# Normalisation of four batches and the turning of two gated weights, moved into the last steps of the head loop

## What is computed

```python
x = x + _L0_attn_ref(_layernorm(x, axis=-1), L0_attn_w_qkv, L0_attn_w_o)      # 16 heads of 128, softmax
x = x + _L0_xattn_ref(_layernorm(x, axis=-1), ctx_2048, ctx_2048, ...)        # linear attention over a context
x = x + _L0_ffn_ref(_layernorm(x, axis=-1), weight1, weight2, weight3)        # gated, NF4 weights
x = x + _L1_attn_ref(_layernorm(x, axis=-1))                                  # over the features
x = x + _L1_xattn_ref(_layernorm(x, axis=-1), ctx_2048, mask_BxS2_bk0, ...)   # masked, gated
x = x + _L1_ffn_ref(_layernorm(x, axis=-1), L1_ffn_c_fc, L1_ffn_c_proj)       # ternary weights
```

```python
q_prime = jax.nn.relu(jnp.einsum('bhnd,fd->bhnf', q, Wqf))
out = jnp.einsum('bhmf,bhfe->bhme', q_prime, kv) / (jnp.einsum('bhmf,bhf->bhm', q_prime, k_sum)[..., None] + 1e-08)
return out.transpose(0, 2, 1, 3).reshape(B, Sq, H) @ Wo.T + bo
```

## Time and profile before

| | |
|---|---|
| median of 3 runs | 932.9 us (932.67 to 932.92) |
| the profiled execution | 934.24 us, its span 932.4 us |
| PE busy | 858.7 us (92% of the span), 6868 matmuls |
| DVE busy | 729.2 us (78%) |
| ACT busy | 520.5 us (56%) |
| POOL busy | 369.0 us (40%) |
| mean granted clock of PE | 0.98 of 2.4 GHz |
| the two parts | DVE's last update of X ends at 564.65 us, ACT's last copy at 567.31 us; the second part's first instruction is at 568.66 us |

### The profile page before, as it was taken

The page is one execution under the profiler, slowest core; times in us unless marked ns, Lnnn a source line. Parts: engine busy times, 40 slices in busy tenths (PEclk is TensorE's granted clock), DMA queues, the critical chain, the costliest instruction groups (busy, mean ns, idle before and its releaser), DMA issues. The chain is left out here.

```text
span 932.4 us, 18697 instructions
## 1 busy us (share of the span) xinstructions
PE 858.7 (92%) x6868; PEld 637.5 (68%) x6868; DVE 729.2 (78%) x1777; ACT 520.5 (56%) x1245; POOL 369.0 (40%) x356
## 2 busy tenths in 40 slices
PE   4798998999999999999999986999988889999786
PEld 3455766777777777777777765787856568777554
DVE  5738867878888788887887745898798879887895
ACT  1435576656665566656665643554364863535556
POOL 3104455545555555545554553044133031522410
PEclk9889999999999999999999997999999999999999
DMA  9022331011101111011100000000000010000001
GB/s 285 32 65 68 55 93 35 2 35 34 34 7 27 34 34 34 0 34 34 34 5 6 1 1 1 1 2 1 1 2 1 1 46 2 1 1 1 1 1 46
DMA packets 34722, 25.56 MB, mean 27 GB/s; under 512 B 9492, under 2 KB 31596, under 8 KB 34668
## 3 DMA queue, kind: packets, MB, share of 16 engines
q1 hardware_dynamic: 34380, 24.56, 10.1%
q10 hardware_dynamic: 288, 0.26, 0.1%
HBM read 22.65 MB, written 2.17 MB: 27 GB/s over the span
## 5 line engine op out<-in xcount | busy, mean ns | idle before, releaser
L476 POOL CAST exp_hi<-exp_scores 128x1024 f16<-128x1024 f32 x64 | 67.0, 1047 | 217.9 <-ACT exp_scores L580 217.9
L74 PE MATMUL banks<-value_out_hi,xn_t_hi 128*128 128x256 f16 x512 | 140.8, 275 | 2.3 <-DVE X L874 2.3
L478 POOL TENSOR_TENSOR exp_lo<-exp_scores,exp_hi 128x1024 f16<-128x1024 f32 x64 | 140.7, 2198 | 5.1
L580 ACT ACTIVATE exp_scores<-banks,exp_bias,unscale 128x256 f32<-128x256 f32 x256 | 141.0, 560 | 2.1
L75 PE MATMUL banks<-value_out_lo,xn_t_hi 128*128 128x256 f16 x512 | 140.6, 275 | 0.0
L76 PE MATMUL banks<-value_out_hi,xn_t_lo 128*128 128x256 f16 x512 | 140.6, 275 | 0.0
L1064 PE MATMUL banks<-qk 128*128 128x256 f32 x512 | 122.7, 383 | 9.9 <-ACT exp_scores L580 9.9
L1064 PEld LDWEIGHTS banks<-qk 128*128 128x128 f32 x512 | 97.2, 191 | 31.4 <-issue 10.5
L874 DVE SCALAR_TENSOR_TENSOR X<-banks,colsum,X 128x256 f32<-128x256 f32 x256 | 106.2, 477 | 11.0 <-DVE colsum L865 9.6
L562 ACT ACTIVATE qk<-banks 128x512 f32<-128x512 f32 x128 | 75.8, 601 | 59.1 <-PE banks L76 59.1
L853 DVE TENSOR_REDUCE neg_rowmax<-banks 128x4 f32<-128x1024 f32 x64 | 78.1, 1221 | 31.4 <-PE banks L1064 31.4
(11 more groups left out here) (238 smaller groups left out, 1965.9 us busy)
## 6 DMA issues: line engine op xcount, KB each, us to landing
head_weights<-in_wqkv_d SPq DMA_DIRECT2D x32, 128.0 KB, 3.7
weight_absmax_rows<-across_partitions SPq DMA_DIRECT2D x15, 256.0 KB, 4.1
X<-in_x_d SPq DMA_DIRECT2D x4, 512.0 KB, 7.5
head_weights<-in_wqkvt_d SPq DMA_DIRECT2D x16, 128.0 KB, 3.4
head_weights<-in_w_o_d SPq DMA_DIRECT2D x16, 128.0 KB, 3.5
out<-X SPq DMA_DIRECT2D x8, 256.0 KB, 2.1
res_then_ternary_then_kv<-in_c_fc_d SPq DMA_DIRECT2D x1, 1024.0 KB, 6.5
res_then_ternary_then_kv<-in_c_proj_d SPq DMA_DIRECT2D x1, 1024.0 KB, 8.2
```

The lines of the kernel that those rows point to most:

```text
L74: nc.tensor.matmul(out, lhs[0], rhs[0], start=first, stop=False)
L476: nc.gpsimd.tensor_copy(probh[:, s1_.par], prob[:, s1_.par]).then_inc(exph_ready, 1)
L478: nc.gpsimd.tensor_tensor(probl[:, s1_.par], prob[:, s1_.par], probh[:, s1_.par], ALU.subtract).then_inc(expl_ready, 1)
L580: last = nc.scalar.activation(prob[:, s1_.par, t, :], sc_ps[t // ST][:, t % ST, :], ACT.Exp, bias=nbias[:, t:t + 1], scale=unscale[:, s1_. ...
```

## The change

Two pieces of work go into the last iterations of the head loop.

1. **Normalisation of batches 0 to 3 for the linear attention.** Pair 0 is final after iteration 62, pair 1 after iteration 63. DVE: statistics of pair 0 in iteration 63 between the reciprocals and the row maxima, its four normalised tiles behind the row maxima; statistics of pair 1 in iteration 64 behind the row maxima, its tiles in iteration 65 between the reciprocals and the column sums. POOL: the powers, on 128x4, at the end of its iterations 62 and 63. The normalised tiles go into `ctxt` and `k0t`, which are free by then. PE turns pair 0 at the end of iteration 64 and pair 1 in iteration 65 between value pass and column sums, eight turns each, into banks 6 and 2. ACT copies each pair with two copies into `g.first_xt`, new room behind kv0's halves. The second part starts with lin_q for streams 0 to 3; the lists of turns leave out their seven stages (`EARLY`), and the waits count from the fifth batch. POOL's addition of bo needs no wait for these four.
2. **The gated weights.** PE turns pieces 0 and 1 in iteration 64 ahead of the scores and pieces 2 and 3 behind the column sums, ahead of the turns of pair 0. ACT copies 0 and 1 ahead of the bias and the exps of that iteration, 2 and 3 behind the copies of pair 0. (The title's "two weights" are w1 and w2.) w3 stays behind the loop, in banks 0 and 1 instead of 2 and 3.

```diff
+EARLY = [f"lin_{part}" for part in ("stats", "aggr", "eps", "pow", "xn", "turn", "xt")]
...
+    first_xn = [t[:, :, :].rearrange("p k n -> p (k n)").rearrange("p (t d) -> p t d", d=D) for t in (ctxt, k0t)]
+    LAST = STEPS - 1
+    FIRST_A, FIRST_B = 6, 2
...
+            for p in range(STREAMS // 2):
+                if known(i) and i == LAST - 1 + p:
+                    pool.wait_ge(early_eps, p + 1)
+                    rows = slice(TP * p, TP * (p + 1))
+                    nc.gpsimd.tensor_tensor(rstd[:, rows], rstd[:, rows], g.neg_half[:, rows], ALU.pow).then_inc(
+                        early_rstd, 1)
...
+            if known(i) and i == LAST + 1:
+                gated_weights(0)
+                gated_weights(1)
             if runs(i, 1):
                 s1_ = Step(i, c - 1)
                 act.wait_ge(nmax_ready, i)
...
+            if known(i) and i == LAST + 1:
+                first_rows(0)
+                gated_weights(2)
+                gated_weights(3)
...
+        def first_rows(p):
+            act.wait_ge(early_full, p + 1)
+            for a in range(2):
+                last = nc.scalar.activation(g.first_xt[2 * p + a],
+                                            bank[(FIRST_A, FIRST_B)[a]].rearrange("p (k n) -> p k n", k=KT), ACT.Copy)
+            last.then_inc(early_xt, 1)
...
+        run(act, step)
+        first_rows(1)
...
+        def first_statistics(p):
+
+            tiles = range(TP * p, TP * (p + 1))
+            dve.wait_ge(x_added, STEPS - NP + p + 1)
+            for t in tiles:
+                nc.vector.bn_stats(stats[:, t, :], g.X[:, t, :]).then_inc(early_stats, 1)
+            dve.wait_ge(early_stats, TP * (p + 1))
+            for t in tiles:
+                nc.vector.bn_aggr(mv[:, t, :], stats[:, t, :]).then_inc(early_aggr, 1)
+            dve.wait_ge(early_aggr, TP * (p + 1))
+            nc.vector.tensor_scalar(rstd[:, TP * p:TP * (p + 1)], mv[:, TP * p:TP * (p + 1), 1], LN_EPS, None,
+                                    ALU.add).then_inc(early_eps, 1)
+
+        def first_rows(p):
+
+            dve.wait_ge(early_rstd, p + 1)
+            for t in range(TP * p, TP * (p + 1)):
+                last = nc.vector.tensor_scalar(first_xn[p][:, t - TP * p, :], g.X[:, t, :], mv[:, t, 0:1],
+                                               rstd[:, t:t + 1], ALU.subtract, ALU.mult)
+            last.then_inc(early_xn, 1)
...
+        def first_rows(p):
+
+            pe.wait_ge(early_xn, p + 1)
+            if p:
+                pe.wait_ge(early_xt, p)
+            else:
+                pe.wait_ge(exp_ready, STEPS)
+            for a in range(2):
+                for t in range(ST):
+                    for k in range(KT):
+                        last = nc.tensor.transpose(bank[(FIRST_A, FIRST_B)[a]][:, k * S + t * P:k * S + (t + 1) * P],
+                                                   first_xn[p][:, a * ST + t, k * P:(k + 1) * P], g.ident[:, :])
+            last.then_inc(early_full, 1)
...
-        pe.wait_ge(lv, ROUNDS * 8 * STEP_OPS)
...
         for q in range(2):
+            pe.wait_ge(wt_ready, 3 + q)
...
-                    last = nc.tensor.transpose(bank[2 + q].bitcast(BF16)[0:rows, at:at + P], src, g.identb[:, :])
+                    last = nc.tensor.transpose(bank[q].bitcast(BF16)[0:rows, at:at + P], src, g.identb[:, :])
...
+    lin_xt = [g.first_xt[b] if b < STREAMS else xt[b] for b in R]
...
+    nl = [b + 1 - STREAMS for b in R]
+    nth_norm = lambda layer, b: nl[b] if layer == "lin" else n[b]
...
-                pe.wait_ge(lin["xt_ready"], n[s])
-                features_first(PB[s], g.wq0, xt[s]).then_inc(lin_q_full, 1)
+                if s >= STREAMS:
+                    pe.wait_ge(lin["xt_ready"], nl[s])
+                features_first(PB[s], g.wq0, lin_xt[s]).then_inc(lin_q_full, 1)
...
+    early = [i for i in range(len(work)) if names[i] in EARLY]
+    done = {(b, i): 0.0 for b in range(STREAMS) for i in early}
+    nth = {(b, e): sum(engine[i] == e for i in early) if b < STREAMS else 0 for b in range(B) for e in ENGINES}
```

More of the change, by code:

```diff
@@ L270, in attention_part @@
     tround, tclamp, tdone = sem("ternary_rounded"), sem("ternary_clamped"), sem("ternary_done")
+    early_stats, early_aggr, early_eps = sem("first_rows_stats"), sem("first_rows_mean"), sem("first_rows_eps")
+    early_rstd, early_xn = sem("first_rows_rstd"), sem("first_rows_xn")
+    early_full, early_xt = sem("first_rows_turned"), sem("first_rows_xt")
+    first_xn = [t[:, :, :].rearrange("p k n -> p (k n)").rearrange("p (t d) -> p t d", d=D) for t in (ctxt, k0t)]
+    LAST = STEPS - 1
+    FIRST_A, FIRST_B = 6, 2
     NF_REP = 12
@@ L595, in step, with gated_weights @@
                                          bias=-ROUND).then_inc(tdone, 1)
-        run(act, step)
-        for w in range(4):
+        def first_rows(p):
[4 more added lines that the diff above has]
+            last.then_inc(early_xt, 1)
+        def gated_weights(w):
             act.wait_ge(wt_full, w + 1)
@@ L607, in _ @@
                 last = nc.scalar.activation(g.w3t[0:rows, k, :],
-                                            bank[2 + q].bitcast(BF16)[0:rows, k % 3 * D:(k % 3 + 1) * D], ACT.Copy)
+                                            bank[q].bitcast(BF16)[0:rows, k % 3 * D:(k % 3 + 1) * D], ACT.Copy)
             last.then_inc(wt_ready, 1)
@@ L842, in step @@
                     nc.vector.reciprocal(rhl[:, s2.par, :, 0], rowsum[:, s2.par, :]).then_inc(rrh_ready, 1)
+            if known(i) and i == LAST:
+                first_statistics(0)
+            if known(i) and i == LAST + 2:
+                first_rows(1)
             if preps(i, c, 2):
@@ L853, in step @@
                 nc.vector.tensor_reduce(nmax[:, :], sc_both, AX.X, ALU.max, negate=True).then_inc(nmax_ready, 1)
+            if known(i) and i == LAST:
+                first_rows(0)
+            if known(i) and i == LAST + 1:
+                first_statistics(1)
             if known(i) and i == 0:
@@ L1432, in norm_stage @@
             elif part == "xn":
[L1433 removed]
+                dve.wait_ge(ln["rstd"], nth_norm(layer, s))
                 for t in range(ST):
@@ L1787, in turns_by_engine @@
     free = {e: 0.0 for e in ENGINES}
-    nth = {(b, e): 0 for b in range(B) for e in ENGINES}
-    done = {}
+    early = [i for i in range(len(work)) if names[i] in EARLY]
+    done = {(b, i): 0.0 for b in range(STREAMS) for i in early}
+    nth = {(b, e): sum(engine[i] == e for i in early) if b < STREAMS else 0 for b in range(B) for e in ENGINES}
     turns = {e: [] for e in ENGINES}
-    for _ in range(B * len(work)):
+    for _ in range(B * len(work) - STREAMS * len(early)):
         best = None
@@ L1851, in decoder @@
     g.kv0 = sb("kv0", [P, B, XH // 2, 34])
-    g.shared = sb("features_then_ternary_then_kv0", [P, 2, F2 * KT])
-    flat = g.shared[:, :, :].rearrange("p a n -> p (a n)").bitcast(F16)
+    halves = B * XH * 17
+    g.many = sb("features_then_ternary_then_kv0_and_rows", [P, halves + STREAMS * KT * S])
+    g.shared = g.many[:, 0:2 * F2 * KT].rearrange("p (a n) -> p a n", a=2)
+    flat = g.many[:, 0:halves].bitcast(F16)
+    g.first_xt = [g.many[:, halves + b * KT * S:halves + (b + 1) * KT * S].rearrange("p (k n) -> p k n", k=KT)
+                  for b in range(STREAMS)]
     g.kvh, g.kvl = (flat[:, n * B * XH * 17:(n + 1) * B * XH * 17].rearrange("p (b j c) -> p b j c", j=XH // 2, c=34)
```

39 lines of the change are left out of this document (20 added, 19 removed).

## The result

The changed kernel takes **921.72 us** (median of 5 runs, 921.54 to 923.28) against 932.9 us before (932.67 to 933.83). The ratio is 0.989, with a 95% interval of 0.9875 to 0.9905: faster by 11.2 us, where 8.7 were forecast. The profiled execution took 921.72 us, its span is 919.9 us.

A forecast was written before the change was run, and what follows sets the result against it. ACT's late w3 copies, then PE up to lin_f1, bound the seam; first part 1.65 us earlier, lin_f1 ending at 579.4 against 588.16, 8.75 us gained: median 924.2 us from 932.9, range 922.4 to 926.8.

The forecast's parts named there:

- What bounds the seam: ACT's w3 copies end the first part last; then PE idles 6.98 us behind DVE's statistics and bounds until lin_f1.
- Iteration 63, +0.3: DVE's pair 0 statistics, 2.2 us in 1.96 us of waiting, move row maxima through ACT's exps by +0.3 us.
- Iteration 64, +0.8: Second statistics, 2.25 us behind the row maxima, make DVE's column sums and PE's last value pass 0.8 us late.
- The value pass, -1.7: PE's last value pass runs at 2.4 GHz because turns fill the gap before it: 1.7 us gained.
- Rival B: Clock lost in the loop's tail too, or low longer behind the barrier: 6.7 us gained, 926.2 us; chance 0.17.
- Iteration 65: DVE's first tensor_scalar waits for POOL's exp_lo; ACT's copies end at 565.65, the first part 1.65 us earlier.
- The barrier, 1.35: Between the parts, from ACT's last copy to DVE's first instruction, the barrier costs 1.35 us.
- The second part: First lin_q matmul at 567.2, 12.2 us of PE to the end of lin_f1 at 579.4: 8.75 us earlier.
- the loss of 1.7: Behind the barrier PE runs 3.4 us at half clock, losing 1.7 us, +0.3 against before.
- The sum: Whole kernel: handover 8.75 us earlier, span 923.7, median 924.2 us.
- from there the same distance to the end (343.6 us): From the handover to DVE to the end of the kernel nothing changes: 343.6 us as before.
- Rival C: Clock does not fall across the barrier: 1.7 us more, 10.4 gained, 922.5 us; chance 0.12.

The follow-up runs named there:

- experiment 4: Changed kernel with pair 0's four bn_stats done twice in iteration 63, first into a spare tile; 924.18 us.
- experiment 5: Changed kernel with pair 1's four tiles normalised on ACT instead of by DVE's four tensor_scalar; 922.53 us.
- experiment 1: The kernel before, unedited, run and traced a second time; 931.26 us.
- experiments 5 and 6: For experiment 5 see its line; 6 is the changed kernel with w3 turns before the last column sums, pair 1's behind: 919.84 us with 20 spare turns, 922.12 without.

## Why the prediction was right or wrong

**What bounds the seam: right.** ACT's copies behind the loop held the first part's end, and the statistics, powers, rows, turns and copies held PE in the second. The parts alone show each by itself: 2.4 us of a and 5.9 us of b.

**Iteration 63, +0.3: wrong, 0.** The four bn_stats and their followers stand from 542.74 to 544.78, 2.04 us, not 2.2, and 0.1 of that is still the wait for the scores: in experiment 4, where nothing else is waited for, they take 1.92 (545.49 to 547.41). I had added 0.1 us for each of two waits, which no row gave, and the rows show 0.02 to 0.04 between the end of one group and the start of the next.

**Iteration 64, +0.8: wrong, +0.1.** The same term. The second statistics stand behind row maxima that are not late, and from the end of these it is 1.84 us to the column sums (552.04 to 553.88) where the idle time had been 1.78. From the start of one row maximum to the column sums of the next iteration it is 9.10 us against 9.03. The +0.8 was a running total that held the +0.3; 0.1 of it came, and the other 0.7 is what the seam gave beyond the forecast (9.4 against 8.75).

**The value pass, -1.7: right.** 2.4 GHz throughout, with a pause of 0.25 us ahead of it. Rival B's first half did not occur in any of the eight traces with both parts, nor in the one with the normalisation only, and did in the one with the weights only, with its pause of 1.38 us. My reason was that a pause of 1.06 us had left the clock high. These pauses fit it, but the pause at the barrier was followed by a fall in one execution and not in another, so the length of a pause alone does not settle it.

**Iteration 65: right.** The first tensor_scalar took 2.25 us against 0.40 for the three behind it. I had it end with POOL's exp_lo plus 0.15; it ended at 558.41, 0.15 after 558.26. Without the block I had put the end of the part 0.65 us earlier, and experiment 5 measured 0.63 without the four. POOL had started 0.03 us before DVE. By the rule of the Trainium skill (SBUF — State Buffer, Who interferes with whom) the one that issues first keeps the port pair for the whole instruction, and the trace agrees: 2.25 us. The other outcome that I had derived from it, DVE first, did not come in any of the eight traces of kernels that have these rows on DVE: their four take 3.21 to 3.22 us in each.

**The barrier, 1.35: half right.** It is 1.35 to 1.41 us from ACT's last copy (before, experiment 1, normalisation only), but DVE itself waits 1.58 to 1.65 us from the end of its last update (changed, weights only, experiments 5 and 6). I had DVE ending 0.25 us ahead of ACT and took ACT's price. In the changed kernel they end 0.08 us apart, and from ACT's end it is 1.56 us: 0.2 more, made up by ACT's end, which was that much earlier against DVE's than forecast.

**The second part: right in its price of the clock, by luck in its sum.** b was forecast as 580.05 - 567.0 = 13.05 us from DVE's first instruction, and is 13.09. Two errors of 0.2 us cancel in it. I had put PE's first matmul 0.2 us behind DVE's first instruction, for a weight load that no row showed by itself, and PE starts with DVE. And I had 12.2 us from there to the end of lin_f1, and it is 12.44 (564.82 to 577.26). Without a half-clock stretch it is 11.41, and it grows by half of the time at half clock: 3.4 us give 13.09, 5.7 give 14.20, 6.1 give 14.42. So the loss of 1.7 was the right price where the clock falls for 3.4 us. (The stretch before lasted longer than the 5.3 us of my bound, which I had counted from PE's first turn: 10.2 us, from 567.81 to 578.05.) Of the eight traces of kernels with both parts, four have that, three have none and one has 6.1 us.

**The sum.** 8.75 forecast, 9.4 found at the seam: the 0.7 between them are the +0.3 and the +0.5 that iterations 63 and 64 were to cost and, but for 0.1, did not. The other 1.8 us of the 11.2 are not in it. The step that failed is the last one, "from there the same distance to the end (343.6 us)". I took 343.6 and the start of iteration 63 as constants of the kernel from a single trace. Each holds a half-clock stretch, worth 1.3 to 1.7 us, that the same kernel does not have in another execution. Rival C, no fall of the clock across the barrier, did happen, in the second trace of the changed kernel, at 11.1 us gained at the seam, and the time was not 1.7 us shorter, since c was 1.6 us longer. In that execution it was no rival for the total.

**Left open.** Why the medians part by 11.2, 10.3 (931.85 - 921.56) and 11.9 us (933.2 - 921.27) in three comparisons, when like traces part by 9.6. The kernel before seems to hold one such stretch more in its median run, as its first trace did (of the stretches above the first holds those at 151 and 697 us, the second neither), but two traces can't give a share. Nor is it shown what makes a stretch come or not at a given place. The three traces of the changed kernel have two behind the barrier each, at 566 and 863, at 685 and 863, and at 567 and 714 us, and so all three have b + c of 354.8 to 355.1; with the statistics twice there are three.

## What to carry to other kernels

Work moved across a barrier pays twice if the engines that end the first part also begin the second: take off each engine's tail what others wait for, and look again at which engine is then last, because two that ended 2.7 us apart may now end together. Price what is put in an idle gap by the rows of the same kind end to end, with no surcharge for waits of an engine on itself, and look at POOL beside every tensor_scalar. Before taking "the rest stays as it is" as a constant, read the rest in two traces of the same kernel: here it differs by 1.5 us, more than most terms of the sum. And where one distance is as long as before, see whether it holds the same things: here the stretch at 714 us seemed to cost nothing only because another was missing.

## What the runs showed of the hardware

- The same pause of PE (3.10 us) is followed by a fall of the granted clock, 0.7 and 1.0 us after PE is back at work, in two traces of the changed kernel, and by none in the third. In the kernel with w3 earlier the clock fell inside the pause, 2.3 us after PE stopped (559.8 to 562.06).
- The half-clock stretches in these traces lasted 3.4, 6.8 or 10.2 us. Laid beside a trace of the same kernel without it, one of 3.4 us cost 1.7 us behind the barrier, 1.6 to 1.7 at 151 us, 1.3 to 1.6 in the masked attention (686 and 697 us), 1.3 at 714 and 1.6 at 863.
- It also comes in the masked attention, in one execution and not in the next. In the second trace of the changed kernel PE had waited 1.76 and 0.63 us, with 0.64 us of work between, before the clock fell at 685.49; in the first trace the same two waits were followed by no fall. At half clock PE is busy for 1.82 and 2.00 us of the 2 us of the rows shown, where the same work at full clock has 1.37.
- DVE's small addition to `headmask`, 0.16 us in experiment 1, took 1.27 us in the changed kernel, where POOL's additions of bo started 0.02 us ahead of it (564.80 and 564.82). With the weights only, where POOL has nothing to do there, it took 0.16 us again. It did no harm in the changed kernel, as DVE had nothing else to do then.
